# A delta-rule attention kernel: the right factor XX gathered by ScalarE instead of GpSimd, and VectorE's halo copies and a tap of v placed ahead of Z plus identity of level 6

## The reference

```python
q = short_conv(x @ Wq, conv_q); k = short_conv(x @ Wk, conv_k); v = short_conv(x @ Wv, conv_v)   # 4 taps, then silu
q = l2norm(q) * SCALE; k = l2norm(k)
g = -exp(A_log) * softplus(x @ Wf1 @ Wf2 + dt_bias)      # one value for each 16 key features
beta = sigmoid(x @ Wb)
def step(S, (qt, kt, vt, gt, bt)):                       # 1024 steps, S is 128 x 128 for each sequence and head
    S = S * exp(gt)
    delta = bt * (vt - kt @ S)
    S = S + kt outer delta
    return S, qt @ S
y = o * silu(x @ Wg + bg); y = y * rsqrt(mean(y * y) + eps) * norm_w;  out = y @ Wo
```

## Time and profile before

| | us |
|---|---|
| median of 3 runs | 5364.82 (5364.24 to 5367.64) |
| the profiled execution | 5359.16 |
| its span, first to last instruction | 5357.3 |
| PE busy | 5145.3 (96%) |
| DVE busy | 4236.8 (79%) |
| ACT busy | 3296.3 (62%) |
| POOL busy | 2080.8 (39%) |

### The profile page before, as it was taken

How to read it: one execution, slowest core, us unless ns; L and a number is a source line. 1 busy time by engine, 2 the same in 40 slices (tenths; PEclk the granted TensorE clock), 3 DMA queues, 4 the chain that set the end, 5 groups by cost and what they waited for, 6 DMA issues and landing times. The chain is left out here.

```text
span 5357.3 us, 87725 instructions
## 1 busy us (share of the span) xinstructions
PE 5145.3 (96%) x27204; PEld 3576.9 (67%) x27204; DVE 4236.8 (79%) x8284; ACT 3296.3 (62%) x6730; POOL 2080.8 (39%) x3561
## 2 busy tenths in 40 slices
PE   4599999999999999999999999999999996999999
PEld 2277777777777777777777777777777775444444
DVE  6699999999999999999999999999999994111110
ACT  3377777777777777777777777777777774010110
POOL 2144444444444444444444444444444442000000
PEclk8799999999999999999999999999999997999999
DMA  2111111111111111111111111111111111222121
GB/s 82 44 29 41 35 41 34 41 33 41 32 40 33 40 32 40 33 40 33 40 33 40 32 40 32 40 33 41 35 42 34 33 32 61 89 91 96 45 71 53
DMA packets 192050, 235.71 MB, mean 44 GB/s; under 512 B 41576, under 2 KB 136424, under 8 KB 187504
## 3 DMA queue, kind: packets, MB, share of 16 engines
q1 hardware_dynamic: 111016, 188.22, 11.8%
q10 hardware_dynamic: 80584, 41.95, 2.7%
HBM read 183.75 MB, written 46.38 MB: 43 GB/s over the span
## 5 line engine op out<-in xcount | busy, mean ns | idle before, releaser
L744 PE MATMUL bank<-xT,weights 128*128 128x512 f32 x4096 | 2089.2, 607 | 32.9 <-PEq L159 32.9
L763 PE MATMUL bank<-KQ,KR 128*128 128x128 f32 x7168 | 998.5, 282 | 13.8 <-DVE KQ L1074 10.4
L1059 DVE SCALAR_TENSOR_TENSOR conv<-pre,taps,conv 128x512 f32<-128x512 f32 x1152 | 974.5, 846 | 22.7 <-ACT conv L1276 8.6
L1513 POOL TENSOR_TENSOR KR<-KR,decay_u 128x256 f32<-128x256 f32 x768 | 669.8, 872 | 813.1 <-PE bank L763 812.2
L763 PEld LDWEIGHTS bank<-KQ,KR 128*128 128x128 f32 x7168 | 878.7, 192 | 24.9 <-DVE KQ L1074 21.7
L1074 DVE TENSOR_TENSOR KQ<-KQ,decay_u 128x512 f32<-128x512 f32 x896 | 824.0, 920 | 30.0 <-PE bank L763 5.2
L744 PEld LDWEIGHTS bank<-xT,weights 128*128 128x128 f32 x4096 | 674.4, 192 | 247.9 <-issue 226.4
L1089 DVE COPY_PREDICATED all_pairs<-level_mask,bank 128x512 f32<-128x512 int32 x896 | 795.4, 888 | 0.0
L1119 DVE TENSOR_TENSOR ZI<-bank,ident_each 128x256 fp32r<-128x256 f32 x768 | 322.4, 420 | 251.0 <-PE bank L795 236.8
L1366 ACT ACTIVATE X<-bank 128x256 fp32r<-128x256 f32 x768 | 297.6, 387 | 361.6 <-PE bank L821 361.2
L1557 POOL CAST XX<-X 128x128 fp32r<-128x128 f32 x640 | 247.9, 387 | 648.5 <-ACT X L1366 629.1
(11 more groups left out here) (197 smaller groups left out, 9396.3 us busy)
## 6 DMA issues: line engine op xcount, KB each, us to landing
decay_u<-decay_scratch SPq DMA_DIRECT2D x128, 510.0 KB
beta_u<-beta_scratch SPq DMA_DIRECT2D x128, 256.0 KB
y_in<-y_scratch SPq DMA_DIRECT2D x32, 1024.0 KB, 4.8
y_scratch<-y_rn ACTq DMA_DIRECT2D x112, 256.0 KB, 2.3
xt<-in_L_attn_hidden_states SPq DMA_DIRECT2D x8, 1024.0 KB, 5.5
x_in<-in_L_attn_hidden_states SPq DMA_DIRECT2D x28, 256.0 KB, 5.0
out<-o_out ACTq DMA_DIRECT2D x28, 256.0 KB, 2.0
w<-in_L_ffn_W SPq DMA_DIRECT2D x8, 704.0 KB, 5.0
```

Source lines behind the costliest of these rows:

```text
L744: last = nc.tensor.matmul(bank[w % 2][:], weights[par][:, w, k, :], xT[:, k, u % J * UC:(u % J + 1) * UC], start=k == 0, stop=k == KC - 1)
L763: last = nc.tensor.matmul(to[:, :, i], KR[:, cols(i)], halves(KQ[m % 2][:, :, cols(i)], l, 1), start=True, stop=True)
L1059: nc.vector.scalar_tensor_tensor(conv[:, w], taps_from(w, t), taps[par][:, w, t:t + 1], conv[:, w], ALU.mult, ALU.add).then_inc(steps.sem, 1)
L1513: nc.gpsimd.tensor_tensor(firsts, firsts, second.to_broadcast([P, 2, UC >> (l + 2), 1 << l]), ALU.mult).then_inc(keys_scaled.sem, 1)
```

## The change

`gather_x` moves from GpSimd to ScalarE and does with two copies what took three: the second copy covers both 128x64 pieces with one pattern. On ScalarE each gather stands right behind `take_x` of the level before. The one of level 1 stands behind `take_delta`. `first_tap(0)` moves from behind the table load to a place ahead of `take_delta`, and `take_right_side` ahead of `round_squares`. On VectorE `add_identity_to_z(6)` moves behind `halo` and `convolve(2, (1,))`, and so behind `last_query` too.

```diff
@@ vector, step
             keep_pairs(4)
-            add_identity_to_z(6)
             last_query()
             halo(z, s.z_first, a, qk_conv_steps, 2 * (TAPS - 1), (0, 1), qk_halo_ready)
             convolve(2, (1,))
+            add_identity_to_z(6)
             scale(5)
@@ scalar
+            def gather_x(u, l, last):
+                if u is None:
+                    return
+                if l >= 2:
+                    wait(act, x_ready, u, l - 1)
+                    wait(act, t_done, u, l)
+                else:
+                    wait(act, x1_ready, u, 1)
+                    if last is not None:
+                        wait(act, t_done, last, LEVELS - 1)
+                nc.scalar.activation(halves(XX[:], l, 1), halves(X[u % 2][:, UC // 2:], l, 1).bitcast(F32), ACT.Copy)
+                to = XX[:].rearrange("p (c m two s) -> p c m two s", c=COUPLES, two=2, s=1 << l)
+                of = X[u % 2][:, 0:UC // 2].rearrange("p (c m two s) -> p c m two s", c=COUPLES, two=2, s=1 << l)
+                nc.scalar.activation(to[:, ::-1, :, 0], of[:, :, :, 0].bitcast(F32), ACT.Copy).then_inc(xx_ready.sem, 1)
@@ scalar, step
             take_x(1)
+            gather_x(b, 2, None)
             keep_z(2)
             take_projection(2)
             take_t(b, 2)
             take_x(2)
+            gather_x(b, 3, None)
             store_output()
             keep_z(3)
             take_t(b, 3)
             take_x(3)
+            gather_x(b, 4, None)
             keep_z(4)
...
             take_x(4)
+            gather_x(b, 5, None)
             take_t(b, 4)
...
             take_x(5)
+            take_right_side()
             round_squares()
-            take_right_side()
             take_x(6)
             take_projection(0)
+            first_tap(0)
             take_delta()
+            gather_x(m, 1, b)
             nc.scalar.preload_act_table_set("natural_log_exp_and_others")
-            first_tap(0)
             inverse_norm()
@@ gpsimd
-            nc.gpsimd.tensor_copy(halves(XX[:], l, 1), halves(natural, l, 1).bitcast(F32))
-            for i in range(COUPLES, B):
-                last = nc.gpsimd.tensor_copy(halves(XX[:, cols(couple(i))], l, 0),
-                                             halves(X[u % 2][:, cols(in_x(i))], l, 0).bitcast(F32))
-            last.then_inc(xx_ready.sem, 1)
```

More of the change, by code:

```diff
@@ L1565, in step @@
                 squares_left(s.a)
-                for l in range(2, LEVELS - 1):
-                    gather_x(s.b, l, None)
                 add_squares(s.c)
@@ L1571, in step @@
             scale_keys(s.m, 1 - s.odd, 0)
-            gather_x(s.b, 2, None)
             scale_keys(s.m, 1 - s.odd, 1)
-            gather_x(s.b, 3, None)
             scale_keys(s.m, 1 - s.odd, 2)
-            gather_x(s.b, 4, None)
             scale_keys(s.m, 1 - s.odd, 3)
-            gather_x(s.b, 5, None)
             scale_keys(s.m, 1 - s.odd, 4)
@@ L1585, in step @@
             out_squares_left(s.c)
-            gather_x(s.m, 1, s.b)
         walk(pool, step)
```

## The result

The changed kernel takes 5377.90 us, median of 13 runs (5373.63 to 5379.19), the kernel before 5364.24 (5358.68 to 5368.32, 13 runs): ratio 1.0024 [1.0016, 1.0033], slower by 0.24%. The forecast was 5386, slower. The profiled execution took 5375.58, its span is 5373.8, 16.5 more than before.

A forecast was written before the change was run, and what follows sets the result against it. PE sets the time, busy 33.01 of 33.02 us a unit, DVE 2.2 behind. +1.3 us a head times 16 heads is +21 on 5359.16, 5380; with 5.7 for the median, 5386 us (chance 0.38), range 5325 to 5418.

The forecast's parts named there:

- Gather on GpSimd, 0.16 us a unit: Behind product level 3 PE waits 0.16 us for XX, held up on GpSimd; moving XX wins that.
- ScalarE free: Ten 128x128 copies of XX, taken as 0.29 us each, stand in ScalarE's 0.70 us holes before Z: cost nothing.
- The store's unit, +0.3 a head: In one unit a head, output stores issue about 0.6 us later, so Z comes late and PE loses 0.3.
- The tap loses against out_sq, Z plus identity comes late: Before level 6 the tap of v starts 0.06 us behind out_sq and waits; PE comes 0.14 later than before.
- a second halo copy that loses its race: In about one unit of three the second halo copy on VectorE also waits, costing 0.13 us: +0.04 a unit.
- Last query, +1.23: Its four small VectorE operations wait for X and GpSimd instructions; PE is 2.1 us late, 0.69 and 0.18 go: +1.23.
- Behind the last query -0.28: In the unit after a head's last query, PE's further 0.28 us of waiting for `delta` is won.
- first chunk +0.1: In a head's first chunk Z plus identity comes 0.6 us late on PE, 0.5 is won back: +0.1.
- A tap that slips in first: Tap starts before out_sq or GpSimd's row stands later; plain unit gains 0.36 us; 5333 us, or 5305; chance 0.30.
- the second rival: DVE's scaling of level 4 stays first, everything behind X is 0.22 us later in seven units: 5411 us; chance 0.12.
- the third: The last query's small operations fit between two GpSimd instructions, its unit costs +0.3 us for +1.23: 5372 us; chance 0.14.
- the fourth: ScalarE is too full: copies take 0.38 us, Z is 0.1 late on four levels: 5430 us and more; chance 0.06.

The follow-up runs named there:

- the gather alone: The changed kernel with VectorE's order as before, leaving XX's move to ScalarE and two small ScalarE moves: 5340.21 us, 0.9953 of the kernel before.
- the third copy: Kernel with only the halo copies ahead of Z plus identity, plus one more 128x128 ScalarE copy per gather into an unread tile: 5333.60 us against 5334.47.
- a short out_sq: The changed kernel with GpSimd's out_sq addition cut from 512 to 4 columns, so the output isn't the reference's: 5293.19 us, 0.9865 of the kernel before.
- the tap before level 5: Kernel with only the halo copies ahead, with the first tap of v moved ahead of Z plus identity of level 5: 5305.74 us, 0.9889 of the kernel before.

## Why the prediction was right

The direction and the mechanism were right; the time came 8 us under the forecast, inside its range.

- **Gather on GpSimd, 0.16 us a unit.** Right: 1.02 became 0.86, and the gather alone gained 23.5 us.
- **ScalarE free.** Right but for the stores' unit, by the gather alone and by the third copy. The copies take 0.31 and 0.29 for the 0.29 taken.
- **The store's unit, +0.3 a head.** The mechanism is right, the size too large: Z does wait for the queue, 0.31 where 0.48 was reckoned, and the unit is 0.11 longer than its plain neighbours (33.09 to 32.98). The queue issued the stores beside the copies, and the second is over 0.19 later, not 0.6.
- **The tap loses against out_sq, Z plus identity comes late.** Right to the 0.06 us of the tap's start and the 0.55 of its end. By the rule of the Trainium skill ("SBUF — State Buffer", "Who interferes with whom") that the pair of ports is locked for a whole instruction this was to be expected; the trace agrees, with 0.54 or 0.55 in four places shown here, and with 0.74 for the same tap once out_sq is short. PE waits 0.34 at level 6 of a plain unit, where 0.30 follows from the prediction (0.14 later in place of 0.16 earlier), and the wait for `delta` gave 0.23 for the 0.18. The 0.04 for a second halo copy that loses its race was wrong: in one unit of three it was to cost 0.13, but it happens in one of eight, and that one takes 32.94, no longer than the others. Plain units gained 0.08, not 0.02.
- **Last query, +1.23.** Right: 34.95 less 33.71 is 1.24, with each of its operations as long as one of GpSimd's. What was missed is the clock: in three of fifteen such units it costs 1.6 us more, 0.34 a head in the mean.
- **Behind the last query -0.28, first chunk +0.1.** Right: -0.32 and +0.14.
- **The sum.** +1.3 a head was forecast, +1.11 measured, and without the clock it would be 0.77: the store's unit and the plain ones were reckoned some 0.5 too dear, and the 0.34 of the clock, which the prediction didn't have, hid most of that. So much of the sum's closeness is luck. In all +21 forecast and +16.5 measured by the spans. Nearly all of the rest of the 8 us is the base: the forecast added 5.7 from the profiled execution to the median, and after the change that distance is only 2.3.
- **The rivals.** A tap that slips in first is what the kernels with a short out_sq and with the tap before level 5 show, and they gain what that rival said and more (5333 or 5305 were given; 5293.19 and 5305.74 are measured). It was not what this change did. The scaling of level 4 lost against the keys in seven units of eight, so the second rival fell; in the eighth, behind the first chunk, it stayed first as that rival has it, at 32.94; the last query was slow, so the third fell; the third copy excludes the fourth.

## What to carry to other kernels

A hole in one engine's timeline is worth little for work that another engine blocks: before work is moved into a hole on VectorE, look at what GpSimd runs there, and count each two-input operation that begins behind one of GpSimd's with the rest of that instruction. A chain of small dependent operations was the dearest thing to put there, 3.00 us for 0.74, since each link waited for a whole instruction. Here one tap placed 2.6 us earlier, before GpSimd's row begins, together with the last query left where it was, made the difference between 0.24% slower and 1.1% faster.

## What was not expected of the hardware

The granted clock fell in some last-query units and not in others, behind the same idle time of PE. Windows of the changed kernel around two such places, the first at 2586.09 (its unit takes 36.55 us), the second at 2853.62 (34.95):

```profile
2586.09:2588.50 2.41, 2.41 (x5) 1.38 (x6) 2.41 (x6) 0.38 (x1) 0.00 (x0) 0.50 0.00 0
2588.50:2589.70 1.20, 1.20 (x10) 1.20 (x8) 0.45 (x1) 1.04 (x2) 0.00 (x0) 0.63 0.00 0
2589.70:2592.30 2.60, 2.60 (x24) 2.56 (x23) 1.00 (x2) 2.20 (x5) 0.85 (x1) 1.00 0.00 0
...
2853.62:2856.09 2.47, 2.47 (x16) 1.99 (x17) 2.47 (x6) 1.44 (x3) 0.00 (x0) 1.00 0.00 0
```
```profile
2853.62 0.44 PE L821 MATMUL bank<-X,ZI 128*128 128x128 f32 x2 [2.04 <-DVE ZI L1119]
2853.89 1.07 PE L744 MATMUL bank<-xT,weights 128*128 128x512 f32 x2
```

Both come behind 2.04 us in which PE waited for the same DVE instruction. In the first the clock is 0.50, which is 1.2 GHz of 2.4, in the 2.41 us that follow, and it is back at 1.00 only after part of the next 1.20: the pair of projections takes 2.02 for 1.07, and the unit 1.6 more. In the second nothing falls. It happened in 3 of the first 15 last-query units of the changed kernel (the last one, where the pipeline runs out, is not counted) and in 8 of 15 of the kernel with only the order changed; in no such unit of the kernel before, where PE doesn't stand idle so long. That is some 5 us of the changed kernel's time. The three are the last queries of the 4th, 9th and 14th head, five heads apart, and at 1254.8, 2586.0 and 3917.2 us; so when the idle stretch falls may have a part in it. What decides between the two outcomes stays open: no run here varied it by itself.
